# Attention scores of a head as one contraction over 96 partitions, its operands stacked by transfers inside the SBUF

## What is computed

```python
x = layernorm(x + self_attention(x))            # 16 query heads, 4 key heads, head size 32, causal
x = layernorm(x + cross_attention(x, ctx))      # 16 heads, head size 32, causal, keys and values from ctx (128 features)
x = layernorm(x + ffn(x))
# either attention, for a head:
att = where(causal, (q @ k.T) / sqrt(32), -inf)
y   = softmax(att) @ v
```

## Time and profile before

| | |
|---|---|
| median of 3 runs | 1054.06 us (1051.56 to 1057.11) |
| span of the profiled execution, first to last instruction | 1048.3 us |
| TensorE busy, mean granted clock | 965.9 us, 0.969 |
| VectorE, ScalarE, POOL busy | 720.1, 524.1, 430.5 us |
| attention phase | 0 to about 600 us |
| one loop iteration | 69.0 us |

### The profile page before, as it was taken

One profiled execution on the slowest core, in us unless ns is written; L12 is line 12 of the kernel. 1 busy time (PEld: TensorE's weight loads), 2 busy tenths in 40 slices (PEclk: granted clock), 3 DMA queues, 4 the chain that ended last, 5 costly groups with the idle time before them and its releaser, 6 DMA issues. The chain is left out here.

```text
span 1048.3 us, 21762 instructions
## 1 busy us (share of the span) xinstructions
PE 965.9 (92%) x7180; PEld 770.8 (74%) x7180; DVE 720.1 (69%) x1640; ACT 524.1 (50%) x1656; POOL 430.5 (41%) x603
## 2 busy tenths in 40 slices
PE   5799999999999999999998788798999999999994
PEld 5587787877877878778767566566777878778773
DVE  3857858769677587695874668788367577567557
ACT  3727547266274473653734343343564564564461
POOL 0223323323133232231230259784076277277376
PEclk9699999999999999999997989899999999999998
DMA  7000000100101001000000077572110100000001
GB/s 266 26 2 2 22 24 0 45 0 0 45 0 45 0 0 45 0 0 27 1 22 1 2 247 236 161 230 71 61 41 2 61 19 10 30 0 20 20 1 40
DMA packets 27628, 47.79 MB, mean 46 GB/s; under 512 B 2752, under 2 KB 8896, under 8 KB 27200
## 3 DMA queue, kind: packets, MB, share of 16 engines
q1 hardware_dynamic: 27584, 47.24, 13.6%
HBM read 39.89 MB, written 4.19 MB: 42 GB/s over the span
## 5 line engine op out<-in xcount | busy, mean ns | idle before, releaser
L220 PE MATMUL bank<-w_ffn,hT 128*128 128x512 f32 x768 | 191.7, 400 | 0.0
L220 PEld LDWEIGHTS bank<-w_ffn,hT 128*128 128x128 f32 x768 | 140.6, 188 | 30.7
L741 PE MATMUL bank<-ident,prob 128*128 128x128 f32 x768 | 115.8, 285 | 12.1 <-DVE probT L586 7.8
L524 ACT ACTIVATE prob<-bank,nmax 128x256 f32<-128x256 f32 x256 | 126.6, 494 | 0.0
L220 PE MATMUL bank<-tile 128*128 128x512 f32 x384 | 99.1, 412 | 20.0 <-DVE tile L1033 20.0
L523 ACT ACTIVATE prob<-bank,nmax 128x128 f32<-128x128 f32 x256 | 97.6, 381 | 22.8 <-DVE nmax L582 22.8
L741 PEld LDWEIGHTS bank<-ident,prob 128*128 128x128 f32 x768 | 87.3, 144 | 27.6 <-issue 16.6
L582 DVE TENSOR_REDUCE nmax<-bank 128x1 f32<-128x256 f32 x256 | 105.5, 412 | 0.0
L425 POOL TENSOR_SCALAR rwide<-rden 128x256 f32<-128x256 f32 x64 | 26.1, 407 | 190.9 <-DVE rden L590 190.3
L1294 ACT ACTIVATE ht<-bank,cols 128x128 f32<-128x128 f32 x192 | 72.4, 457 | 62.5 <-PE bank L1431 62.5
L220 PEld LDWEIGHTS bank<-tile 128*128 128x128 f32 x384 | 72.7, 195 | 41.9 <-DVE tile L1033 16.8
(11 more groups left out here) (136 smaller groups left out, 1913.0 us busy)
## 6 DMA issues: line engine op xcount, KB each, us to landing
raw<-in_ent_wT SPq DMA_DIRECT2D x32, 256.0 KB, 3.3
raw<-in_ent_pw SPq DMA_DIRECT2D x32, 256.0 KB, 3.7
x<-in_xT SPq DMA_DIRECT2D x8, 512.0 KB, 4.5
xres<-in_x SPq DMA_DIRECT2D x8, 512.0 KB, 3.4
aux<-in_path_w SPq DMA_DIRECT2D x8, 512.0 KB, 3.4
out<-y SPq DMA_DIRECT2D x16, 256.0 KB, 2.0
xb<-x SPq DMA_DIRECT2D x3, 1024.0 KB, 5.1
aux<-in_gate_w SPq DMA_DIRECT2D x8, 256.0 KB, 2.7
```

What stands on the lines that cost most here:

```text
L220: ins = t.matmul(out, lhs(a, k), rhs(b, k), start=first and n == 0 and m == 0, stop=last and n == len(kts) - 1 and m == 2, skip_group_chec ...
L524: k.drain(("S", i, j), s.activation(prob[:, slot, P:PW], bank[:, P:PW], ACT.Exp, bias=nmax[:, slot, 1:2], accum_out=den[:, i % 2, j, 1:2]))
L741: ins = t.transpose(bank[:, c * P:(c + 1) * P], prob[:, (i % 2) * HG + j, c * P:(c + 1) * P], ident[:, :])
```

## The change

**Layout.** The columns of the key and query weights are reordered so that in a projection's output partition 4d + j holds feature d of head j (before: partition 32j + d).

**Stacking.** A projection of `sk`, `sq`, `ck` or `cq` is written, high and low part, into one of four slots of `stage`. Then SP's queue issues three transfers inside the SBUF, each of a whole part (128 partitions of 256 values), into 32 partitions of four heads: for queries high, low, high; for keys high, high, low. A head's contraction over these 96 partitions is the sum of the three partial products.

**Scores.** A head is then a mask product and two products, one for each query tile. `query_tile` goes.

**Buffers.** Stacked queries have a ring of 3 (`q3`), stacked cross keys a ring of 2 (`kc3`), the self keys one (`ks3`). `sqT`, `skT`, `cqT`, `ckT` go. `prob` and `probT` have six slots in place of eight: two heads of each have only one, so that ScalarE waits for the transposes of the second head before it writes it again. `x1T` shares memory with `oT_cross` instead of `oT_self`.

**Order.** In a body with both attentions the groups go: self 0, 1, 2, cross 0, self 3, cross 1, 2, 3. The list becomes: `ck0 sq1`, step 0, `wo0 wo1 sv0 sv1 sq2`, step 1, `x1t0 x1t1 cq0`, step 2, `cq1 cv0 cv1 sq3`, step 3, `cq2 ck1`, step 4, `cq3 ck2`, step 5, `ck3`, step 6, `sk0`, step 7, `sq0`, steps 8 and 9, `wout0 wout1`. In the last body: `ck0 wo0 wo1 ck1 x1t0 x1t1 cq0 cq1 cv0 cv1`, step 0, `cq2 ck2`, step 1, `cq3 ck3`, steps 2 to 5, `wout0 wout1`.

**SP's queue.** Its loads of the next context and x now stand at the start of a body, the load of x for the residual at its end, behind all stackings and behind the last normalisation. Before a stacking it waits until the target's last scores have been read by the maxima (`scored`).

The core of the diff (`Stages` counts each slot's transfers: `wait_slot` waits until a slot's last transfers are done, `wait_moved` for an item's own):

```diff
 def groups_of(cross, nxt):
-    return (list(range(NG)) if cross else []) + (list(range(NG, 2 * NG)) if nxt else [])
+    if cross and nxt:
+        return [NG, NG + 1, NG + 2, 0, NG + 3, 1, 2, 3]
+    return list(range(NG)) if cross else list(range(NG, 2 * NG))
...
+    if cross and nxt:
+        ev = [("ck", 0), ("sq", 1)]
+        after = {0: [("wo", 0), ("wo", 1), ("sv", 0), ("sv", 1), ("sq", 2)],
+                 1: [("x1t", 0), ("x1t", 1), ("cq", 0)],
+                 2: [("cq", 1), ("cv", 0), ("cv", 1), ("sq", 3)],
+                 3: [("cq", 2), ("ck", 1)],
+                 4: [("cq", 3), ("ck", 2)],
+                 5: [("ck", 3)]}
+        if proj:
+            after[6], after[7] = [("sk", 0)], [("sq", 0)]
+        after[n + 1] = [("wout", 0), ("wout", 1)]
+    elif cross:
+        ev = [("ck", 0), ("wo", 0), ("wo", 1), ("ck", 1), ("x1t", 0), ("x1t", 1), ("cq", 0), ("cq", 1), ("cv", 0), ("cv", 1)]
+        after = {0: [("cq", 2), ("ck", 2)], 1: [("cq", 3), ("ck", 3)], n + 1: [("wout", 0), ("wout", 1)]}
     else:
+        ev = [("sq", 1), ("sv", 0), ("sv", 1), ("sq", 2)]
+        after = {0: [("sq", 3), ("weights", 0)], 1: [("weights", 1)], n - 1: [("sk", 0)], n + 1: [("sq", 0)]}
...
+Q_RING, K_RING, N_STAGE = 3, 2, 4
+LOADS = 3 * 16
+def stage_slots(cross, nxt, proj):
+    if cross and nxt:
+        slots = {("ck", 0): 0, ("sq", 1): 1, ("sq", 2): 2, ("cq", 0): 3, ("cq", 1): 0, ("sq", 3): 1, ("cq", 2): 2,
+                 ("ck", 1): 3, ("cq", 3): 0, ("ck", 2): 1, ("ck", 3): 0, ("sk", 0): 3, ("sq", 0): 2}
...
+            def stack(k, moved, kind, i, dst):
+                k.wait_drained((kind, i))
+                q.sem_inc(s_passed, 1)
+                slot = moved.slot((kind, i))
+                for r, part in enumerate((0, 0, 1) if kind in ("sk", "ck") else (0, 1, 0)):
+                    q.dma_start(dst[r * HD:(r + 1) * HD, :, :].bitcast(F32), stage[:, slot, part, :].bitcast(F32)).then_inc(s_stage[slot], 16)
+            def scored(b, groups, i):
+                done = b * (2 * NG) + NG if i is None else group_number(b, groups, i)
+                wait_alone(q, s_max, done * HG, s_passed)
...
+            def staged(k, b, moved, kind, i):
+                moved.wait_slot(s, b, (kind, i))
+                hi(k, (kind, i), stage[:, moved.slot((kind, i)), 0, :], SCALE if kind in ("sq", "cq") else 1.0)
...
                 def scores(i):
...
+                    if (groups[i] < NG or g > 0) and (i > 0 or not nxt):
+                        moved.wait_moved(t, b, ("cq" if groups[i] < NG else "sq", g))
+                    if groups[i] < NG:
+                        moved.wait_moved(t, b, ("ck", g))
+                    kh = kc3[0:K3, g % K_RING, :, :] if groups[i] < NG else ks3[0:K3, :, :]
+                    qh = q3[0:K3, i % Q_RING, :, :]
+                    for j in range(HG):
+                        k.wait_free(("S", i, j))
+                        bank = banks[plan.bank(("S", i, j))]
+                        diag = bank[:, :].rearrange("p (a b c) -> p a b c", a=2, b=2)[:, :, 0, :]
+                        t.matmul(diag, ident16[:, :], mask16[:, :, :], start=True, stop=False, skip_group_check=True)
+                        t.matmul(bank[:, 0:P], qh[:, j, 0:P], kh[:, j, 0:P], start=False, stop=False, skip_group_check=True)
+                        k.filled(("S", i, j), t.matmul(bank[:, P:PW], qh[:, j, P:S], kh[:, j, 0:S], start=False, stop=True, skip_group_check=True))
```

More of the change, by code:

```diff
@@ new lines, with __init__, after, loop @@
+class Stages:
+    def __init__(self, sems):
+        self.sems = sems
+        self.base, self.per, self.count, self.at = [0] * len(sems), [0] * len(sems), [0] * len(sems), {}
+    def after(self, it=0):
+        p = Stages(self.sems)
+        p.base = [b + it * n + c for b, n, c in zip(self.base, self.per, self.count)]
+        return p
+    def loop(self):
+        self.per = list(self.count)
+        return self
+    def fill(self, cross, nxt, proj):
+        for name, slot in stage_slots(cross, nxt, proj):
+            self.take(name, slot)
+        return self
+    def take(self, name, slot):
+        self.count[slot] += 1
+        self.at[name] = (slot, self.count[slot])
+    def slot(self, name):
+        return self.at[name][0]
+    def wait_moved(self, eng, it, name):
+        slot, k = self.at[name]
+        eng.wait_ge(self.sems[slot], it * (LOADS * self.per[slot]) + LOADS * (self.base[slot] + k))
+    def wait_slot(self, eng, it, name):
+        slot, k = self.at[name]
+        if self.base[slot] + k > 1:
+            eng.wait_ge(self.sems[slot], it * (LOADS * self.per[slot]) + LOADS * (self.base[slot] + k - 1))
+    def wait_begun(self, eng, it, slot):
+        eng.wait_ge(self.sems[slot], it * (LOADS * self.per[slot]) + LOADS * self.base[slot])
@@ L290, in attention_phase @@
     s_hi = sem("s_hi")
+    s_stage = [sem(f"s_stage{i}") for i in range(N_STAGE)]
     s_max = sem("s_max")
@@ L317, in attention_phase @@
     attention_plan(plan_7, *LAST)
+    moved_pro = Stages(s_stage)
+    moved_pro.take(("sk", 0), 3)
+    moved_pro.take(("sq", 0), 2)
+    moved_first = moved_pro.after().fill(*FIRST)
+    moved_loop = moved_first.after().fill(*LOOP).loop()
+    moved_6 = moved_loop.after(B - 3).fill(*SECOND_LAST)
+    moved_7 = moved_6.after().fill(*LAST)
+    MOVED = {FIRST: moved_first, LOOP: moved_loop, SECOND_LAST: moved_6, LAST: moved_7}
     def every_iteration(eng, body):
@@ L388, in _ @@
+            every_iteration(q, body)
         @block.gpsimd
@@ L700, in body @@
             def body(b, plan, cross, nxt, proj):
-                k = Banks(t, plan, b)
+                k, moved = Banks(t, plan, b), MOVED[cross, nxt, proj]
                 groups = groups_of(cross, nxt)
-                def query_tile(bank, qT, kT, g, qt, heads):
-                    for x, y in ((0, 0), (0, 1), (1, 0)):
-                        last = []
-                        for j in heads:
-                            rows = slice(HD * j, HD * (j + 1))
-                            last.append(t.matmul(bank[j][:, P * qt:P * qt + P * (qt + 1)], qT[rows, x, g, qt * P:(qt + 1) * P],
-                                                 kT(y)[rows, 0:P * (qt + 1)], start=False, stop=qt == TT - 1 and (x, y) == (1, 0), skip_group_check=True))
-                    return last
@@ L714, in scores @@
                 def scores(i):
                     g = groups[i] % NG
-                    qT, kT = (cqT, lambda h: ckT[:, h, g, :]) if groups[i] < NG else (sqT, lambda h: skT[:, h, :])
-                    own = [plan.bank(("S", i, j)) for j in range(HG - 1)]
-                    for name in ([("cq", g), ("ck", g)] if groups[i] < NG else [("sq", g)] if g > 0 else []):
-                        if plan.bank(name) not in own:
-                            k.wait_drained(name)
-                    bank = [banks[plan.bank(("S", i, j))] for j in range(HG)]
@@ L726, in scores @@
-                    for heads in (range(HG - 1), [HG - 1]):
-                        for j in heads:
-                            k.wait_free(("S", i, j))
-                            diag = bank[j][:, :].rearrange("p (a b c) -> p a b c", a=2, b=2)[:, :, 0, :]
-                            t.matmul(diag, ident16[:, :], mask16[:, :, :], start=True, stop=False, skip_group_check=True)
-                        query_tile(bank, qT, kT, g, 0, heads)
-                    for j, ins in enumerate(query_tile(bank, qT, kT, g, 1, range(HG))):
-                        k.filled(("S", i, j), ins)
+                    if i == 0:
+                        moved.wait_begun(t, b, 2)
+                        if nxt:
+                            moved.wait_begun(t, b, 3)
```

169 lines of the change are left out of this document (92 added, 77 removed).

## The result

The changed kernel takes 1120.28 us (median, 1116.88 to 1122.31) beside 1053.17 of the kernel before on the same chip: ratio 1.064, 95% interval 1.060 to 1.067. Slower was right; the size was not: forecast 1078, range up to 1100.

A forecast was written before the change was run, and what follows sets the result against it. TensorE, busy for 92% of the span, was taken as the bound. Per iteration idle +5.95, scores -5.4, clock +2.9 us; times seven 24.2, so the span becomes 1072.5 and the forecast 1078 us, range 1060 to 1093, with rivals 1050 to 1100.

The forecast's parts named there:

- (e): Stack transfers on SP's queue: three land 3.7 us after the low part; covered except `ck2`, 0.4 us idle an iteration.
- R3: Rival: transfers land at 5.1 us instead of 3.0, making `ck1`, `ck2` and `ck3` late; 1096 us, chance 0.10.
- the line on the first and last iteration: Both gain 0.67 us a step, but the last's `cq3` and `ck3` land some 1.9 late; taken as 0, 3 either side.
- R5: Rival: the 96-row score block is no shorter than 2.12 us; 1116 us, chance 0.03.
- (a): End of the iteration, steps 8 and 9 adjacent and `wout` at once: 1.34 and 0.31 us idle, 1.65 together.
- (b): Start of the iteration: step 0's fourth head waits for `ck0`'s bank, its low part behind `wout1`'s normalisation on VectorE; 1.45 us.
- (c): Step 1: the fourth transposes wait for a VectorE copy behind two maxima; 0.35 us.
- (d): After step 1: `cq0` waits for x1, whose high parts stand behind ScalarE's exponentials; 3.4 us idle in every iteration.
- R2: Rival, faster: `cq0`'s wait is hidden, so 3.4 and 2.9 us go each iteration; 1034 us, chance 0.17.
- Clock: Behind (d)'s idle the clock falls to 1.2 GHz in each iteration; price 2.9 us, between 2.44 and 3.4.
- R1: Rival: the clock stays up, leaving 0.55 us for each of seven iterations; 1058 us, chance 0.15.
- R4: Rival: a second clock fall in each iteration, from (a) and (b), 3.1 us idle within some 12; 1098 us, chance 0.07.

The follow-up runs named there:

- e6: Kernel before in its own order, scores as one mask product and two of 96 rows from constants, nothing transferred: 1015.27 us, ratio 0.965.
- e2: Changed kernel with all transfers issued, but scores computed from constant weight columns, so no score waits for a stack: 1061.09 us, ratio 1.009.
- e1: New order of groups and projections with the old 32-row scores and no transfers, against the kernel before: 1118.47 us, ratio 1.063.
- e3: Changed kernel with `cv0`, `cv1` and `sq3` moved between `x1t1` and `cq0`: 1096.53 us, ratio 1.043 to the kernel before.
- e5: e2 with the 312 transfers left out as well: 1063.77 us, ratio 1.011 to the kernel before.
- e9: e8 with `ck0 sq2` ahead of `wo0 wo1` and `sk0` one step later: 1082.62 us, ratio 1.028 to the kernel before.
- e12: e8 with only `sq1` first, `ck0 wo0 wo1 sv0 sv1 sq2` behind step 0, `ck2` behind step 3, last body reordered: 1076.17 us, ratio 1.024.
- e14: Changed kernel with projections up to `cq1` in one stretch ahead of the steps, groups reordered, stacks two steps ahead, high parts issued first: 1098.84 us, ratio 1.044.
- e8: Changed kernel with another projection order and each stack's two high-part transfers issued before its low part is written: 1063.23 us, ratio 1.012 to the kernel before.
- e15: Kernel before in its own order, only self groups scoring over 96 rows from transferred stacks, high parts first: 1047.53 us, ratio 0.996.
- e16: e15 with `sq2`, `sq3`, `sk0` let go once TensorE has written the old stack's scores, and `sq3` ahead of the first step 0: 1043.58 us, ratio 0.993.

## Why the prediction was wrong in size

Two steps failed, about equally, and a third a little.

The first is (e), the transfers. It took SP's issue as 0.35 us from a load out of DRAM; a transfer inside the SBUF takes 0.6 (median 0.595), three 1.84. The landing was nearly right, 3.0 in the sum and 3.3 in the median. `ck1` was walked as having 0.6 to spare and came 2.15 late; of these 2.75, 2.2 are the later second stack (6.9 against 4.75), and the rest was not traced. Step 6 or 7 waits 0.9 to 1.5, step 1 in two iterations 0.7 and 0.9, and the seventh iteration has 2.2 besides. That is 2.8 to 4.8 us an iteration in place of 0.4. R3, the rival for late transfers (1096, chance 0.10), had the wait but blamed the landing.

The second is the line on the first and last iteration. "I take 0, with 3 us to both sides"; measured 17.1. The wait of the first two steps 0 for their stacks (4.43 and 3.89) wasn't walked, nor the load of x for the last body. For the last body the prediction named `cq3` and `ck3`; the late one was `ck2`, 3.30, and step 3 behind it did not wait.

The third is small: 5.4 us for the scores had 0.67 for all eight steps, although the text had said that VectorE leaves a pure step 0.2. Busy time at full clock is 63.3 where 67.7 less 5.4 is 62.3; e6 has 63.4. So 4.4.

Per iteration, over the first six of the windows (mean 76.6, busy 66.8, so 9.75 idle against 1.3): idle +8.5 against +5.95 forecast; scores -4.4 against -5.4; clock 66.8 less 63.3, +3.5 against +2.9. Sum +7.6 against +3.45. The whole difference of the spans, 69.7, is the forecast's 24.2, another 26.8 in the seven iterations, 17.1 around them and 1.6 behind.

One reading of the prediction is off without weight in the sum: in the earlier trace rows the clock is low in two slices behind 600 us as well, and not only at the ends of the attention phase.

What held, point by point:

- Scores: 0.36 a head, 1.43 a block. R5 fell. e6 and e2 against e1 (57 us apart) show the new products to be the shorter ones. The Trainium skill (TensorE: Matmul & The Clock Gate, Part 3: Packing small matmuls — row/col tiling) gives a factor of 3.07 for four row groups at 512 columns, by which the old ones would have been; these products of 128 and 256 columns don't reach it.
- (a) 1.34 + 0.31, forecast 1.65. (b) 1.31, forecast 1.45 (in six iterations; the first has no `wout` ahead of it). (c) 0.25, forecast 0.35. (d) 3.20, forecast 3.4, at the named place and by the named cause; e3 took it away and 24 us with it. R2 fell.
- Clock: the mean price came near, 3.5 against 2.9, but not by the mechanism, so that is luck. The clock was to fall behind (d) each time. In the iteration at 150 it never fell: `cq0` took 1.62 behind the same 3.20. In the one at 303 it fell in three places, and the price was 5.8: behind (b)'s 1.31 (granted 0.62 from 306.0 to 310.5), behind (d), and behind step 5's 2.15 (granted 0.53 from 350.59 to 354.0). The Trainium skill (same page, Why this matters for your kernels) advises against idle gaps above about 3 us between bursts; here gaps of 3.2 were followed by either level, and some of 1.31 and 2.15 by the lower one. Nor do the waits alone set the price: e2 and e5 have the same (a) to (d) and no waits on stacks, and their iterations, cut alike, are busy 63.0 to 64.6 in the one and 62.9 to 68.7 in the other. Why one iteration keeps the clock and the next does not stays open. R1 (it stays up) and R4 (a second fall) each describe some iterations.

Three attempts to mend the order (e9, e12, e14) missed by 23 to 54 us, in the same way as the forecast: a moved item was counted for the wait that it removes, and not for the cover that it takes from the place it leaves, or for the queue (VectorE's, SP's) that it brings in front of another. Not tried: e8 with its first and last iterations mended, where by the rows above its loss lies; more places for key stacks, fewer and longer transfers for a stack, and issuing from a second engine's queue.

## What to carry to other kernels

When an operand has to be moved before use, walk each such operand from the write of its last part through the issuing queue, with issue times taken from a transfer of the same kind, to its landing, the second of a pair above all; and do it for the first and last iteration by themselves. An order in which one engine runs almost without idle time is worth keeping as a start: e6, e15 and e16 changed scores inside the old order and came out ahead, while every kernel with another order came out behind. That doesn't show that another order must lose: e8's iterations are 0.9 us shorter than before, and what stands around them gives more than that back. A shorter TensorE block pays in full only where other engines are not already pacing the step; here a pure step gave 0.3 of 0.69 us.

## What the runs showed of the hardware

- SP takes 0.6 us to issue a transfer of 128 KB within the SBUF (each row 1 KB), where a load of 128 KB from DRAM takes 0.35. The six of two stacks held its queue for 3.9 us (343.43 to 347.29).
- The transfers' traffic, a DMA share of 0.39 in e2's iterations against 0.05 in e5's, changed neither the time of the kernel nor the mean length of an exponential (0.495 in both), a maximum (0.412) or a copy (0.547).
- After the same idle time of 3.2 us the 12 products that follow took 1.62 us in one iteration and 2.90 in another; after 1.31 us, 24 products of 512 columns took 7.36 in one and, after 1.37, 5.77 in another.
